# Two best experts and their ranks made tile by tile in the layers, with the last five tiles left to the router

## What is computed

```python
xn = _layernorm(x)
x = x + gnn(xn, edge_index, edge_weight, ...) + linear_attention(xn[None], ...)[0]
x = x + moe(_layernorm(x)[None], ...)[0]

# gnn: agg[d] = sum over edges (s, d) of norm * (xn @ W)[s]; h = layernorm(agg + ...); relu(0.5 * h + 0.5 * xn)
# moe, with E = 16 experts and K = 2:
gate_logits = x @ gate_w + gate_b
topk_vals, topk_idx = jax.lax.top_k(gate_logits, K)
topk_w = jax.nn.softmax(topk_vals, axis=-1)
h = jax.nn.relu(jnp.einsum('bsh,ehf->bsef', x, w1) + b1)
expert_out = jnp.einsum('bsef,efh->bseh', h, w2) + b2
moe = sum over the two chosen experts of topk_w * expert_out
y = layernorm(x + moe)
```

## Time and profile before

| | us |
|---|---|
| median of 3 runs | 1805.78 (1800.36 to 1808.45) |
| the profiled execution | 1800.89, its span 1799.1 |
| layers, first gather to the last aggregate | 220.9 to 1217.8 |
| router, first step to the experts' first step | 1230.0 to 1298.7 |
| experts, to the last output | 1298.7 to 1799.1 |
| busy over the span | PE 83%, POOL 59%, DVE 55%, ACT 30% |

### The profile page before, as it was taken

The page is one execution under the profiler, slowest core; times in us unless marked ns, Lnnn a source line. Parts: engine busy times, 40 slices in busy tenths (PEclk is TensorE's granted clock), DMA queues, the critical chain, the costliest instruction groups (busy, mean ns, idle before and its releaser), DMA issues. The chain is left out here.

```text
span 1799.1 us, 34047 instructions
## 1 busy us (share of the span) xinstructions
PE 1490.5 (83%) x7872; PEld 1211.9 (67%) x7873; DVE 983.1 (55%) x3365; ACT 531.1 (30%) x1463; POOL 1065.6 (59%) x1116
## 2 busy tenths in 40 slices
PE   7999778777978786977887779873499999999987
PEld 4676566565757565755765557652289989988976
DVE  8999466534466453742755347266833333343457
ACT  3444422111211121211211112110055555555523
POOL 2332477777777777777777777760045545545545
PEclk9999879986978898898889979876699999999989
DMA  8010533333333333333333333337432233254266
GB/s 277 28 36 24 164 103 106 106 103 105 104 105 103 104 104 105 102 105 105 103 103 104 105 102 105 104 101 144 114 110 77 72 118 94 73 182 131 70 233 232
DMA packets 105305, 200.76 MB, mean 112 GB/s; under 512 B 24384, under 2 KB 59840, under 8 KB 105248
## 3 DMA queue, kind: packets, MB, share of 16 engines
q0 software_dynamic: 48336, 132.17, 25.3%
q1 hardware_dynamic: 56624, 67.29, 12.2%
q10 hardware_dynamic: 288, 0.66, 0.1%
HBM read 166.44 MB, written 33.60 MB: 111 GB/s over the span
## 5 line engine op out<-in xcount | busy, mean ns | idle before, releaser
L786 POOL DMA_INDIRECT ring<-table,staged x784 | 746.1, 952 | 242.5 <-issue 229.4
L1061 PE MATMUL bank<-ring,hots 128*128 x1372 | 325.0, 392 | 50.3 <-SPq L775 50.3
L1061 PEld LDWEIGHTS bank<-ring,hots 128*128 128x128 f32 x1372 | 266.0, 196 | 100.6 <-issue 63.6
L1458 POOL DMA_INDIRECT got_x<-rows,at_x x114 | 110.2, 967 | 201.9 <-DVE at_x L1576 178.5
L1061 PE MATMUL bank<-ring,late_hots 128*128 x388 | 138.5, 506 | 98.2 <-SPq L775 89.6
L1553 PEld LDWEIGHTS bank<-xT,w 128*128 128x128 f32 x1696 | 207.1, 193 | 15.4 <-issue 10.2
L1553 PE MATMUL bank<-xT,w 128*128 128x128 f32 x1696 | 208.3, 276 | 8.6 <-issue 8.6
L1526 ACT ACTIVATE hT<-bank,b 128x128 f32<-128x128 f32 x424 | 155.7, 367 | 181.4 <-PE bank L1553 156.9
L1561 PE MATMUL bank<-w,hT 128*128 128x256 f32 x848 | 201.1, 380 | 2.3 <-DVE y L1618 2.2
L1061 PEld LDWEIGHTS bank<-ring,late_hots 128*128 128x128 f32 x388 | 90.2, 248 | 140.4 <-issue 126.5
L871 DVE TENSOR_SCALAR hots<-iota_t,edge_l 128x128 f32<-128x128 f32 x686 | 181.8, 363 | 1.8
(11 more groups left out here) (278 smaller groups left out, 2287.4 us busy)
## 6 DMA issues: line engine op xcount, KB each, us to landing
w<-in_w SPq DMA_DIRECT2D x32, 512.0 KB, 4.9
ring<-table,staged POOLq DMA_INDIRECT x784
got<-spread SPq DMA_DIRECT2D x11, 1024.0 KB, 8.1
rows<-xn SPq DMA_DIRECT2D x1, 6272.0 KB, 28.6
out<-out_c SPq DMA_DIRECT2D x12, 512.0 KB, 3.9
xt<-in_x_cols SPq DMA_DIRECT2D x11, 512.0 KB, 3.5
table<-xn SPq DMA_DIRECT2D x6, 896.0 KB, 6.5
x<-in_x SPq DMA_DIRECT2D x4, 896.0 KB, 11.2
```

Of the source, the lines that this page charges most:

```text
L786: pool.indirect_dma_start(out=ring[:, j, :], out_offset=None, in_=a.table, in_offset=bass.IndirectOffsetOnAxis(ap=staged[:, half, col:col ...
L1061: last = nc.tensor.matmul(agg, hot[:, k, :], two[:, k, :], start=False, stop=False)
L1458: pool.indirect_dma_start(out=got[:, n, :], out_offset=None, in_=a.rows, in_offset=bass.IndirectOffsetOnAxis(ap=at[:, n:n + 1], axis=0)).t ...
```

## The change

In the layers DVE's turn t gets `top_two` for tile t - 6 (for the tiles 0 to 43): ten steps over 16 elements that make the two one-hot rows `m.one`, the two largest logits (into `m.share`) and their sum `m.both`. It stands after the chain of x1 and before the wait for the aggregate. PE's small block in the turn after multiplies `m.both` by the triangle and by ones, and DVE's small block then adds the running totals `m.run` to the ranks, writes them over the tile's logits, and makes the next running totals. For this the turns written out at the start go on to turn 7.

In the router the choosing steps run over the LEFT = 5 last tiles only. PE makes the totals first and the ranks after, one product each of 80 columns; DVE adds the five totals one after the other, and the ranks of the five tiles once. The pass over all tiles that made running sums, and the two additions of ranks before the places, are gone. The gates are made behind the places instead of beside the products. The one-hot matrices are now 16-bit. Memory is shared differently: xT and hT of the experts lie where `m.one` was.

```diff
+ROUTED = NT - 5
+    m.one = sb("one", [P, 2, NT, E], F16)
+    m.both = sb("both", [P, NT - ROUTED, E])
+    m.run = sb("run_e", [P, 2, E])

+def top_two(dve, c, m, t, score, pick, rest, both):
+
+    down = m.const[:, C_DOWN:C_DOWN + E]
+    of = tile(m.logits, t, E)
+    for k in range(2):
+        best, one = tile(m.share, t, 2)[:, k:k + 1], tile(m.one[:, k], t, E)
+        c.add(dve.reduce_max(best, of, axis=AX.X))
+        c.wait()
+        settle(dve, m)
+        c.add(dve.scalar_tensor_tensor(score, of, best, down, ALU.is_equal, ALU.mult))
+        c.wait()
+        settle(dve, m)
+        c.add(dve.reduce_max(pick, score, axis=AX.X))
+        c.wait()
+        settle(dve, m)
+        c.add(dve.tensor_scalar(one, down, pick, None, ALU.is_equal))
+        c.wait()
+        settle(dve, m)
+        if k == 0:
+            c.add(dve.scalar_tensor_tensor(rest, one, -3e38, of, ALU.mult, ALU.add))
+            c.wait()
+            settle(dve, m)
+        of = rest
+    return dve.tensor_tensor(both, tile(m.one[:, 0], t, E), tile(m.one[:, 1], t, E), ALU.add)

 # layers(), the vector engine's turn, between the chain of x1 and that of h
+                if routed(t, 6):
+                    top_two(dve, Count(dve, chain_top, (t - 6) * CHAIN_TOP, CHAIN_TOP), m, t - 6, score[:], pick[:], rest[:],
+                            m.both[:, n, :]).then_inc(both_ok, 1)
 # its small block, behind the addition that makes the logits of tile t - 5
+                    if routed(t, 7):
+                        dve.tensor_tensor(tile(m.logits, t - 7, E), rank_ps, m.run[:, n, :], ALU.add)
+                        dve.tensor_tensor(m.run[:, o, :], total_ps, m.run[:, n, :], ALU.add)
 # the tensor engine's small block, behind the gate product
+                    if routed(t, 7):
+                        pe.wait_ge(both_ok, t - 6)
+                        nc.tensor.matmul(rank_ps, m.tri, m.both[:, 1 - n, :], start=True, stop=True)
+                        done = nc.tensor.matmul(total_ps, m.ones, m.both[:, 1 - n, :], start=True, stop=True)
-        FIRST_TURN, UNROLLED, LAST_TURN = -3, 3, NT + 4
+        FIRST_TURN, UNROLLED, LAST_TURN = -3, 4, NT + 4

 # route(): the selecting steps on LEFT = NT - ROUTED tiles
-            down = m.const[:, C_DOWN:C_DOWN + E][:, None, :].broadcast_to([P, NT, E])
+            down = m.const[:, C_DOWN:C_DOWN + E][:, None, :].broadcast_to([P, LEFT, E])
...
-            dve.wait_ge(eg_ok, 1)
-            c.add(dve.tensor_scalar(gap[:], eg[:], 1.0, None, ALU.add))
-            c.wait()
-            c.add(dve.reciprocal(m.share[:, :, 0], gap[:]))
-            c.wait()
-            dve.tensor_tensor(m.share[:, :, 1], eg[:], m.share[:, :, 0], ALU.mult).then_inc(gates_ok, 1)
...
-            for k, (t0, t1) in enumerate(SPLIT):
-                c.add(dve.tensor_copy(both[:, t0:t1, :], total_ps[k][:, 0:t1 - t0, :]))
-            c.wait()
-            c.add(dve.tensor_copy(pre[:, 1:NT, :], both[:, 0:NT - 1, :]))
-
-            here = pre
-            by7 = here[:].rearrange("p (g j) e -> p g j e", j=7)
-            for j in range(1, 7):
-                c.wait()
-                c.add(dve.tensor_tensor(by7[:, :, j, :], by7[:, :, j, :], by7[:, :, j - 1, :], ALU.add))
-            c.add(dve.memset(group[:, 0, :], 0.0))
-            for g in range(1, NT // 7):
-                c.wait()
-                c.add(dve.tensor_tensor(group[:, g, :], group[:, g - 1, :], by7[:, g - 1, 6, :], ALU.add))
-            c.wait()
-            c.add(dve.tensor_tensor(by7, by7, group[:, :, None, :].broadcast_to([P, NT // 7, 7, E]), ALU.add))
-            c.wait()
-
-            c.add(dve.tensor_tensor(cnt[:], here[:, NT - 1, :], both[:, NT - 1, :], ALU.add))
-            c.wait()
+            run = m.run[:, (ROUTED + 7) % 2, :]
+            here = m.logits
+            for k in range(LEFT):
+                c.add(dve.tensor_tensor((ran[:, k + 1, :] if k < LEFT - 1 else cnt[:]), run, total_ps[:, k, :], ALU.add))
+                c.wait()
+                run = ran[:, k + 1, :] if k < LEFT - 1 else None
             c.add(dve.tensor_scalar(nb[:], cnt[:], 1.0, float(BLOCK - 1), ALU.max, ALU.add))
+            dve.wait_ge(rank_ok, 2)
+            c.add(dve.tensor_tensor(here[:, ROUTED:NT, :], rank_ps, ran[:], ALU.add))
             c.wait()
...
-            for k, (t0, t1) in enumerate(SPLIT):
-                c.add(dve.tensor_tensor(here[:, t0:t1, :], here[:, t0:t1, :], rank_ps[k][:, 0:t1 - t0, :], ALU.add))
-            c.wait()
             for k in range(2):
-                c.add(dve.tensor_tensor(score[:], here[:], one[k][:], ALU.mult))
+                c.add(dve.tensor_tensor(score[:], here[:], m.one[:, k], ALU.mult))
...
+            dve.wait_ge(eg_ok, 1)
+            c.add(dve.tensor_scalar(gap[:], eg[:], 1.0, None, ALU.add))
+            c.wait()
+            c.add(dve.reciprocal(m.share[:, :, 0], gap[:]))
+            c.wait()
+            dve.tensor_tensor(m.share[:, :, 1], eg[:], m.share[:, :, 0], ALU.mult).then_inc(gates_ok, 1)
...
             pe.wait_ge(both_ok, 1)
-            for k, (t0, t1) in enumerate(SPLIT):
-                nc.tensor.matmul(rank_ps[k][:, 0:t1 - t0, :], m.tri, both[:, t0:t1, :], start=True, stop=True)
-                last = nc.tensor.matmul(total_ps[k][:, 0:t1 - t0, :], m.ones, both[:, t0:t1, :], start=True, stop=True)
-            last.then_inc(rank_ok, 1)
+            nc.tensor.matmul(total_ps, m.ones, m.both[:], start=True, stop=True).then_inc(rank_ok, 1)
+            nc.tensor.matmul(rank_ps, m.tri, m.both[:], start=True, stop=True).then_inc(rank_ok, 1)

 # experts(): two buffers now lie where m.one was
-        xT = sb("xT", [P, DC, BLOCK])
-        hT = sb("hT", [P, FC, BLOCK])
+        free = m.one[:].rearrange("p k t e -> p (k t e)").bitcast(F32)
+        xT = free[:, 0:DC * BLOCK].rearrange("p (c n) -> p c n", c=DC)
+        hT = free[:, DC * BLOCK:(DC + FC) * BLOCK].rearrange("p (c n) -> p c n", c=FC)
```

More of the change, by code:

```diff
@@ L701, in layers @@
         mark = sb("mark", [P, 1])
+        score = sb("score_l", [P, E])
+        rest = sb("rest_l", [P, E])
+        pick = sb("pick_l", [P, 1])
         rows_i = sb("rows_i", [1, 9, NT + 1], I32)
@@ L762, in on, with routed @@
             return not isinstance(t, int) or 0 <= t - back < NT
+        def routed(t, back):
+            return not isinstance(t, int) or 0 <= t - back < ROUTED
         def later(t, least):
@@ L821, in _ @@
             c.add(dve.memset(mv[:], 1.0))
+            c.add(dve.memset(m.run[:], 0.0))
             c.add(dve.memset(var[:], 1.0))
@@ L1162, in moe @@
         SLOTS = 4
+        m.places = ctx.enter_context(nc.sbuf_tensor("places", [P, NT, 2], I32))
+        m.list = ctx.enter_context(nc.sbuf_tensor("list", [P, BLOCKS + 4, 2], I32))
+        m.lists = ctx.enter_context(nc.sbuf_tensor("lists", [1, 2, E], I32))
+        m.which = ctx.enter_context(nc.sbuf_tensor("which", [P, BLOCKS + 4, 2], F32))
         e = Names()
@@ L1192, in route @@
         HALVES = ((0, 4), (4, 7))
-        best = sb("best", [P, 2, NT])
-        pick = sb("pick", [P, NT])
+        LEFT = NT - ROUTED
+        pick = sb("pick", [P, LEFT])
         score = sb("score", [P, NT, E])
[L1196 to L1200, removed]
+        rest = sb("rest", [P, LEFT, E])
         gap = sb("gap", [P, NT])
@@ L1204, in route @@
         cnt = sb("cnt", [P, E])
+        ran = sb("ran", [P, LEFT, E])
         nb = sb("nb", [P, E])
@@ L1254, in _ @@
             c.add(dve.tensor_copy(of_tile[:], m.iota[:, 0:NT, None].broadcast_to([P, NT, 2])))
-            down = m.const[:, C_DOWN:C_DOWN + E][:, None, :].broadcast_to([P, NT, E])
+            down = m.const[:, C_DOWN:C_DOWN + E][:, None, :].broadcast_to([P, LEFT, E])
+            some = score[:, 0:LEFT, :]
             for k in range(2):
-                of = (m.logits, rest)[k]
-                c.add(dve.reduce_max(best[:, k, :], of[:], axis=AX.X))
+                of = (m.logits[:, ROUTED:NT, :], rest[:])[k]
+                best, one = m.share[:, ROUTED:NT, k], m.one[:, k, ROUTED:NT, :]
+                c.add(dve.reduce_max(best, of, axis=AX.X))
@@ L1260, in _ @@
                 c.wait()
[L1261 removed]
+                c.add(dve.tensor_tensor(some, of, best[:, :, None].broadcast_to([P, LEFT, E]), ALU.is_equal))
                 c.wait()
[L1263 removed]
+                c.add(dve.tensor_tensor(some, some, down, ALU.mult))
                 c.wait()
[L1265 removed]
+                c.add(dve.reduce_max(pick[:], some, axis=AX.X))
@@ L1271, in _ @@
                     c.wait()
-            dve.tensor_tensor(both[:], one[0][:], one[1][:], ALU.add).then_inc(both_ok, 1)
-            dve.tensor_tensor(gap[:], best[:, 1, :], best[:, 0, :], ALU.subtract).then_inc(gap_ok, 1)
-            dve.wait_ge(eg_ok, 1)
-            c.add(dve.tensor_scalar(gap[:], eg[:], 1.0, None, ALU.add))
-            c.wait()
-            c.add(dve.reciprocal(m.share[:, :, 0], gap[:]))
-            c.wait()
```

(1 more changed line is left out.)

29 lines of the change are left out of this document (12 added, 17 removed).

## The result

| | before | after |
|---|---|---|
| median of the runs beside each other | 1807.07 (1800.36 to 1808.45) | 1792.85 (1791.31 to 1793.36) |
| ratio | | 0.9927, 95% interval 0.9901 to 0.9954 |
| the profiled execution, its span | 1800.89, 1799.1 | 1793.25, 1791.4 |
| h of tile 48 (DVE) | 1217.79 | 1224.45 |
| router's first step on the logits | 1231.04 | 1238.38 |

In the medians the change gains 14.2 us, by the ratio 13 (8 to 18). The profiled pair shows 7.7, because before's profiled execution, 1800.89, lies near that kernel's lowest, 1800.36. The forecast was 1795.1, a gain of 10.7. To the experts' first gather the profiled pair gains 10.05 us; the experts then lose 2.35.

The account below looks back on a forecast made before the run. POOL's gathers were taken to pace the layers at 20 us a tile, one dependent DVE chain the router. Router -18.1 plus layers +7.4 gave -10.7 us, from the median 1805.8 to 1795.1; range 1785 to 1807.

Parts of the forecast that it names:

- Selecting steps (a): Router: eleven choosing steps and the sum shrink to 80 elements, 12.05 us to 3.2, gain 8.8.
- Totals and ranks (b): Router, from both to nb_i: one product of 80 columns, five chained adds and the rank addition; 11.4 us to 2.3, gain 9.1.
- Rank additions and gates (c, d): Router: two rank additions before score go, 1.06 us; the gates move onto the path, +0.86.
- Router, sum: All router terms together: -8.8 - 9.1 - 1.1 + 0.9 = -18.1 us.
- Layers: Small steps added to DVE's turns are hidden until tile 46, then uncovered at the stage's end: +7.4 us.
- T: Time top_two and the two additions add to a DVE turn: 3.4 us in turns written out, 4.0 in the loop.
- The rule on small VectorE tiles: Layers: the skill's fixed latency speaks against small steps; its table's 0.08 us a step would hide everything, sum -18.
- Rest: Extra unrolled turns, memset and reused memory: nothing on the path; POOL under 1 us, hidden by the late DVE.
- Rival 1: Layers: the gather ring fills when T is large; gain used up at T = 5.1; chances 0.06 not slower, 0.07 slower.
- My hand recurrence: Layers: lateness carried by hand over two-late-pair tiles; POOL not held up to T = 4.9, loses 16 us at 5.2.
- Rival 3: Router's end meets the transfers, or the layers' tail loses its PE cover: 4 us go, 1799; chance 0.13.

Follow-up runs that it names:

- second profile: The changed kernel run again with no edit, beside the kernel before on the same chip: median 1792.07 us against 1803.69, ratio 0.9947.
- Nine left: Changed kernel with nine tiles instead of five left to the router, so no top_two stands behind turn 45: 1786.82 us, ratio to before 0.9907.
- the layers alone: Layers' part of the changed kernel with the router of the kernel before, which chooses again for all 49 tiles: 1812.57 us, ratio to before 1.0041.
- the one at T = 4.8: Kernel with nine tiles left to the router, plus three repeated steps in each top_two: median 1790.98 us of four runs.
- the third place: Changed kernel with a third place in late_hots, so DVE builds a tile's second late pair without waiting for PE: 1786.89 us.

## Why the prediction was right

- **Selecting steps (a).** Forecast 12.05 to 3.2 us; measured 1241.64 - 1238.38 = 3.26.
- **Totals and ranks (b).** Forecast 11.4 to 2.3; measured 1243.83 - 1241.64 = 2.19. The product of totals, priced at 0.8 between two far bounds, lasts 0.72.
- **Rank additions and gates (c, d).** Forecast -0.2 together; from nb_i to part_e 8.95 became 8.72. The store of the shares is issued 14.3 us after the router's start instead of 13.4; 0.8 was forecast.
- **Router, sum.** Forecast -18.1; -17.4 in the first pair, -17.5 by the second profile. Up to part_e it is -18.3; 0.9 is lost behind that, 0.6 of it in the wait for PE's last list product, 1.61 instead of 0.98 us, with a granted clock of 0.55 instead of 0.69 over the lists. This was no step of mine.
- **Layers.** Forecast T 3.4 in the last turns and 4.0 in the loop, h of tile 48 at 1224.9 without a wait, +7.4 at the stage's end. Measured 3.3 to 3.5 and 3.8, 1224.45, +7.34. T in the loop is 3.8 instead of 4.0: a top_two takes 3.6 there, 0.3 more than in the last turns. Nine left shows the place, the layers alone show the sign.
- **The rule on small VectorE tiles.** The Trainium skill ("VectorE: DVE Perf Modes", The TRN2 errata) says that every instruction pays a fixed latency, so that many small tiles pay it many times. The trace agrees in kind, but the estimate from its table, 0.08 us a step, would have made the layers free. The same section of the Trainium skill says that this row of the table falls short, and gives (N + 151)/0.96 ns for an fp32 addition of N elements; the estimate from that is 0.17, 0.24 and 0.97 us for 16, 80 and 784 elements, and the rows have 0.17, 0.24 and 0.97, so the prediction quoted the weaker of the two figures, and rightly did not go by it. The steps of top_two started 0.28 to 0.42 apart, 0.17 to 0.27 without the increment. Layers alone at +8.9 shows that they were not free.
- **Rest.** POOL under 1 us: from first to last gather 989.85 us instead of 988.95. The experts were taken as unchanged; they differ by +2.35 in this pair and by up to 7 between profiles of any kernels. This scatter, more than a step of the sum, is the distance between 10.7 and 7.7 or 13; the first gather of the experts, ahead of it, came 10.05 us earlier. That the sum is so near is in part luck: in the layers h of tile 48 came 6.7 us later instead of 7.1, and the tail behind it grew by 0.7 instead of 0.3.
- **Rival 1 was mis-sized.** "POOL is not held up to T = 4.9 in the loop" failed: two of five profiles with T = 3.8 have a wait of 3 us at 541 or 542, and the one at T = 4.8 has a wait of 2. My hand recurrence had one PE pace; PE's place at tile 13 varies by 6 us between executions. Those two profiles have their last gather at 1212.9 and 1214.5 instead of 1210.2 to 1210.7; in the changed kernel, where DVE is the late one at the end, part of that is hidden (h of tile 48 with the layers alone 1225.63 instead of 1224.9). At the upper end the recurrence was too steep: it gave some 26 us at T = 5.3 (15 slower than before, and the gain), and measured are 18 to 19 at 5.7. So 19 for the expected 20 is luck, a T read too low against a cost worked out too high. Where the whole gain is lost is known only as between T = 4.8 and 5.7 in nine left.
- **Rival 3** named the transfers, or a tail that loses PE's cover. Transfers don't end the router: the experts' first gather waits for DVE's at_x, as in the kernel before, and PE's first product of the experts comes 6.4 us behind it (before 6.3). The tail from h of tile 48 to the router's start is 13.9 instead of 13.3 us in the changed kernel; in the profile of the third place it is 17.4, 3.5 more than in the changed kernel.

## What to carry to other kernels

Work added to an engine with long waits is free only while a later wait is still to come: forty small blocks cost under 1 us, the last four cost 7, and leaving those four tiles to the next stage, which costs 1.8 there, gained 5 in all. A wait that puts an engine a whole turn late uses up the slack of the following turns; with it removed (one more buffer) blocks half as long again cost under 2 us instead of 18. When the late engine is made punctual, look at what the other one then does: in one profile here PE went idle and came back at half its clock.

## What was unexpected of the hardware

- A semaphore increment of its own between two dependent 16-element steps on DVE costs 0.12 us (3.28 against 2.16 for nine of them), over half of the 0.2 between steps without it.
- An idle of 4.47 us on PE was followed by 12 us at a granted clock of 0.50. With 36 products of zeros in that place, 4.09 us, the clock was 1.00 (in a kernel that also has longer steps).
- Executions whose instructions up to there are the same meet tile 13's second late pair between 506 and 512.5 us, the changed kernel itself at 506.5 and 509.6.
- One chip ran the kernel before 21% slower, with gaps of 1.5 to 2.4 us on PE put down to "issue".
